# The order of calls in the ticks of every engine, drawn anew, in a software pipeline on one core

## What is computed

```python
x = x + rwkv_block(layernorm(x))     # 4 layers: time mix with a scan, channel mix 128 -> 512 -> 128
x = x + ffn(layernorm(x))            # gate, up 128 -> 352, down 352 -> 128, operands rounded to fp4
x = x + attention(layernorm(x))      # one causal head of 64 channels, softmax, output 64 -> 128
x = x + ffn(layernorm(x))

# in each layer of rwkv_block, k, v, r being products with mixes of h and h one token back:
#   out = (e1 * aa + e2 * v) / (e1 * bb + e2);  aa, bb: sums that decay, pp: their running maximum
# fp4: 16 neighbouring values share a scale, max|x| / 6, and are rounded to a grid of 8 magnitudes
```

## Time and profile before

| | us |
|---|---|
| time, median of 3 runs (1369.5 to 1373.78) | 1373.0 |
| span of the profiled execution (the time less what lies around it) | 1368.5 |
| PE busy | 1303.0 |
| ACT busy | 1257.6 |
| DVE busy | 1238.3 |
| POOL busy | 1122.6 |

### The profile page before, as it was taken

One profiled execution on the slowest core, in us unless ns is written; L12 is line 12 of the kernel. 1 busy time (PEld: TensorE's weight loads), 2 busy tenths in 40 slices (PEclk: granted clock), 3 DMA queues, 4 the chain that ended last, 5 costly groups with the idle time before them and its releaser, 6 DMA issues.

```text
span 1368.5 us, 23485 instructions
## 1 busy us (share of the span) xinstructions
PE 1303.0 (95%) x7285; PEld 935.9 (68%) x7285; DVE 1238.3 (90%) x2169; ACT 1257.6 (92%) x2539; POOL 1122.6 (82%) x1216
## 2 busy tenths in 40 slices
PE   3799999999999999999999999988999998899997
PEld 1356677667766677667766677766777876677776
DVE  6999999999999999999999999569999577978994
ACT  6899999999999999999999999877887899998884
POOL 6888998888888888888899999979998465666784
PEclk9899999999999999999999999999999999999999
DMA  7000000000000000000000000010000000000011
GB/s 237 1 1 1 1 1 1 1 21 13 1 0 2 1 1 1 1 1 1 1 1 1 8 24 21 27 32 1 1 1 1 2 1 1 1 16 16 24 32 39
DMA packets 26923, 18.54 MB, mean 14 GB/s; under 512 B 1072, under 2 KB 26160, under 8 KB 26800
## 3 DMA queue, kind: packets, MB, share of 16 engines
q1 hardware_dynamic: 26800, 17.05, 4.2%
HBM read 12.85 MB, written 4.19 MB: 12 GB/s over the span
## 4 chain that ended last, share of the span: by engine, by line
PE 67%; ACT 11%; DVE 9%; POOL 6%; issue 5%; DMA 0%; SPq 0%; DVEq 0%; ACTq 0%; POOLq 0%
PE ps L1154 12%; PE ps L1137 12%; PE ps L1213 5%; PE ps L1037 4%; PE ps L1192 4%; PE ps L1185 4%; PE ps L1144 3%; PE ps L1124 3%; PE ps L1089 3%; PE ps L1090 3%; PE ps L1102 3%; PE ps L1082 3%; PE ps L1263 3%; PE ps L1201 2%; PE ps L1245 2%
## 5 line engine op out<-in xcount | busy, mean ns | idle before, releaser
L1137 PE MATMUL ps<-xk,W 128*128 128x512 f32 x512 | 250.7, 593 | 1.4 <-ACT kf L864 1.4
L1154 PE MATMUL ps<-W,kf 128*128 128x128 f32 x2048 | 249.6, 275 | 0.0
L754 ACT ACTIVATE z<-X,ln_rs 128x128 f32<-128x128 f32 x512 | 239.7, 720 | 3.7 <-POOL ln_rs L603 3.7
L1154 PEld LDWEIGHTS ps<-W,kf 128*128 128x128 f32 x2048 | 239.2, 192 | 2.3 <-issue 1.0
L864 ACT ACTIVATE kf<-ps 128x512 f32<-128x512 f32 x256 | 186.6, 817 | 0.5 <-PE ps L1137 0.5
L871 ACT ACTIVATE kf<-kf 128x1024 f32<-128x1024 f32 x128 | 164.6, 1286 | 0.0
L1037 PEld LDWEIGHTS ps<-idn,z 128*128 128x128 f32 x664 | 83.1, 143 | 113.3 <-issue 87.3
L1137 PEld LDWEIGHTS ps<-xk,W 128*128 128x128 f32 x512 | 91.9, 190 | 92.1 <-issue 89.0
L710 POOL TENSOR_TENSOR W<-W,hsc 128x704 f32<-128x704 f32 x64 | 88.8, 1388 | 59.0 <-DVE W L493 58.8
L1037 PE MATMUL ps<-idn,z 128*128 128x128 f32 x664 | 102.0, 277 | 29.8 <-ACT z L754 20.7
L601 POOL TENSOR_TENSOR ln_rs<-ln_rs,mhalf 128x8 f32<-128x8 f32 (+1 forms) x70 | 127.9, 1827 | 0.0
(11 more groups left out here) (176 smaller groups left out, 3962.5 us busy)
## 6 DMA issues: line engine op xcount, KB each, us to landing
X<-x_in SPq DMA_DIRECT2D x16, 256.0 KB, 6.9
xi<-x_in SPq DMA_DIRECT2D x16, 256.0 KB, 2.9
out<-X SPq DMA_DIRECT2D x16, 256.0 KB, 2.3
W<-weights SPq DMA_DIRECT2D x4, 832.0 KB, 8.4
W<-fp4w SPq DMA_DIRECT2D x1, 560.0 KB, 3.8
row<-rows SPq DMA_DIRECT2D x1, 192.0 KB, 2.9
wqkv<-qkv SPq DMA_DIRECT2D x1, 96.0 KB, 5.7
idn<-ident SPq DMA_DIRECT2D x1, 64.0 KB, 3.1
```

The costliest lines, as they stand in the source:

```text
L754: last = e.activation(chunk(dst, j), chunk(src, j), ACT.Identity, bias=rs[:, 1, j:j + 1], scale=rs[:, 0, j:j + 1])
L1137: e.matmul((pF0, pF1)[f % 2][:, :], w_of(r, WCK + f), xk[r % 2][:, :], start=True, stop=True).then_inc(kf_mm[f], 1)
L1154: last = e.matmul(chunk(pKV, j), kf[r % 3][:, f, j * 128:(j + 1) * 128], w_of(r, WCV + f), start=f == 0 and j == 0, stop=f == 3, skip_grou ...
```

## The change

All functions stay as they are: the same instructions, tiles and waits. Drawn anew are the order of the calls in the four loops over ticks and, for some, the number taken off `t`. All loops now begin one tick earlier, at `FIRST = -1`, and end three earlier. Of the four tables two pieces stand here, the end of PE's old one and its successors in the new, and two edits of DVE's:

```diff
-TICKS = FFN2_AT + 35
+TICKS = FFN2_AT + 32
+FIRST = -1
...
-            for t in range(TICKS):
+            for t in range(FIRST, TICKS):
...
-                similarity(att_job(t - 6), 3)
-                a_turn(att_job(t - 4))
-                h_turn(ffn_job(t - 8), 2)
-                f_up(ffn_job(t - 5), 0)
-                p_values(att_job(t - 7))
...
+                p_values(att_job(t - 8))
+                output(t - 9)
+                f_gate(ffn_job(t - 6), 1)
+                f_up(ffn_job(t - 6), 0)
...
-                init_stats(t)
+                init_stats(t + 1)
```

More of the change, by code:

```diff
@@ L551, in vector @@
                 sub_d(t - 5)
[L552 removed]
+                rwkv(t - 7)
+                mul_up(ffn_job(t - 5), 1)
+                fh_add(ffn_job(t - 6), 0)
+                mix_k(t - 9)
                 bn2(t - 8)
[L554 to L561 removed]
@@ L575, in vector @@
-                prepare(t - 2)
-                weights_rounded(t - Q_AT - 3)
-                fh_scale(ffn_job(t - 5))
-                mix_k(t - 9)
-                fh_add(ffn_job(t - 6), 1)
+                mul_up(ffn_job(t - 5), 2)
+                fh_sub(ffn_job(t - 6), 0)
+                prepare(t - 3)
+                mul_up(ffn_job(t - 5), 3)
+                arg_r(t - 5)
+                a_mask(att_job(t - 5), 0)
+                fx_scale(ffn_job(t - 2))
+                a_max(att_job(t - 5), 0)
@@ new lines, in vector @@
+                fh_max(ffn_job(t - 5))
+                fx_inverse(ffn_job(t - 2))
+                fh_scale(ffn_job(t - 5))
+                mix_t(t - 4)
+                fh_add(ffn_job(t - 6), 1)
+                fh_inverse(ffn_job(t - 5))
+                fh_sub(ffn_job(t - 6), 1)
+                a_mask(att_job(t - 5), 1)
+                a_max(att_job(t - 5), 1)
+                init_stats(t + 1)
+                init_affine(t - 1)
+                a_inverse(att_job(t - 6))
+                a_mask(att_job(t - 5), 2)
@@ L585, in gpsimd @@
+                weights_scales(t - Q_AT + 18)
+                fx_max(ffn_job(t - 1))
+                gate(t - 11)
+                add_xa(t - 7)
+                a_add(att_job(t - 6))
+                bn1(t - 1)
+                fx_add(ffn_job(t - 2))
+                scan_pp(t - 4)
+                mul_up(ffn_job(t - 4), 0)
+                gated(t - 5)
+                fx_sub(ffn_job(t - 2))
+                mul_u(t - 6)
         def gpsimd():
@@ L722, in gpsimd @@
             constants()
-            for t in range(TICKS):
-                sub_dh1(t - 6)
-                add_res(ffn_job(t + 4))
-                mul_y(t - 9)
-                weights_divided(t - Q_AT - 2)
-                a_rsqrt(att_job(t - 5))
-                fh_scaled(ffn_job(t - 9), 0)
-                scaled_p(t - 9)
-                add_bias(att_job(t - 8))
-                add_num(t - 8)
-                fx_scaled(ffn_job(t - 6))
-                fx_divided(ffn_job(t - 5))
-                fh_divided(ffn_job(t - 8), 0)
-                fh_scaled(ffn_job(t - 9), 1)
-                add_den(t - 8)
-                add_xb(t - 14)
-                sub_dh(t - 11)
-                rsqrts(t - 4)
-                init_rsqrt(t - 2)
-                fh_divided(ffn_job(t - 8), 1)
-                f_rsqrt(ffn_job(t - 2))
-                weights_scaled(t - Q_AT - 5)
+            for t in range(FIRST, TICKS):
+                weights_divided(t - Q_AT - 5)
+                add_res(ffn_job(t - 2))
+                add_den(t - 16)
+                fx_scaled(ffn_job(t - 13))
+                sub_dh(t - 19)
+                add_bias(att_job(t - 14))
+                scaled_p(t - 16)
+                a_rsqrt(att_job(t - 11))
+                fh_scaled(ffn_job(t - 16), 0)
+                add_xb(t - 22)
+                rsqrts(t - 12)
+                weights_scaled(t - Q_AT - 19)
+                fx_divided(ffn_job(t - 12))
+                fh_divided(ffn_job(t - 15), 0)
+                fh_scaled(ffn_job(t - 16), 1)
+                f_rsqrt(ffn_job(t - 9))
+                mul_y(t - 16)
+                init_rsqrt(t - 9)
+                sub_dh1(t - 13)
+                fh_divided(ffn_job(t - 15), 1)
+                add_num(t - 15)
         def scalar():
@@ L982, in scalar @@
             prepare_vectors()
-            for t in range(TICKS):
+            for t in range(FIRST, TICKS):
+                square(t - 12, 0)
+                keep_hq(ffn_job(t - 9), 2)
+                fx_magic(ffn_job(t - 4))
+                norm1(t - 4)
+                silu(ffn_job(t - 6), 1)
+                tanh_r(t - 7)
+                square_1(t - 8)
+                fh_magic(ffn_job(t - 7), 0)
+                keep_h2(t - 10)
+                keep_fx(ffn_job(t - 5))
+                init_z(t - 1)
+                relu(t - 11, 1)
+                seeds(t - 7)
+                silu(ffn_job(t - 6), 2)
+                relu(t - 11, 2)
+                silu(ffn_job(t - 6), 3)
```

142 lines of the change are left out of this document (49 added, 93 removed).

## The result

The changed kernel takes 1419.99 us (median of 4, 1418.99 to 1423.17) against 1371.29 for the kernel before in the same comparison (median of 4): a ratio of 1.0353, 95% interval 1.0334 to 1.0372. The prediction was 1370.3 in a range of 1364.5 to 1379. The profiled execution has a span of 1418.9, 50.4 more than before.

A forecast was written before the change was run, and what follows sets the result against it. PE was taken to set the recurrent rounds, DVE the fill and first FFN, a ring of waits the join. Terms −4.7 + 1.9 − 1.1 + 0.5 + 0.7 + 0 = −2.7 on span 1368.5, plus 4.5: 1370.3 us, range 1364.5 to 1379.

The forecast's parts named there:

- Part 6: Recurrent rounds: PE's and ACT's sums unchanged and a new POOL–ACT ring of 12.84 under 13.11, so 0 us.
- the ring through POOL: Recurrent rounds: waits from ACT's h through POOL's sub_dh, two additions and root to ACT's norm2 and h; 12.84 us.
- the sign that the prediction named for being wrong: Recurrent rounds: a round longer than 13.11, with ACT's norm2 waiting for POOL's root.
- Rival B: Recurrent rounds: slower, the POOL–ACT ring sets the round; +7.5 beside −2.7, 1377.8 us, or about 1380; chance 0.18.
- point of decision: Recurrent rounds: the POOL–ACT ring sets the round if it is 0.3 us longer than summed.
- Part 1: Join of attention and second FFN: f_up 0 behind f_gate 1 shortens 8 ticks from 17.88 to 17.28; −4.7 us.
- Part 2: Start: DVE takes X2's statistics before the first affine and idles 1.7 longer for the transfer; +1.9 us.
- Part 3: From the rounds to the first FFN: fx_max moves into DVE's idle time and add_res comes a tick earlier; −1.1 us.
- the two terms of the forecast: Rounds to first FFN: fx_max in DVE's idle time, −0.6; POOL's add_res one tick earlier, −0.5.
- Part 4: DVE, FFN ticks: a lost gap between mul_up 3 and fh_max costs 0.04 in each of 24 ticks; +0.5 us.
- Part 5: Recurrent rounds: POOL's fp4 weight scaling, moved 4 to 6 ticks, overruns a round's slack once or twice; +0.7 us.

The follow-up runs named there:

- e10: The changed kernel with POOL's scaled_p moved from between sub_dh and the root to behind mul_y; 1418.56 us, ratio 1.0338.
- e5: The changed kernel with DVE's mix_rt moved directly behind mix_r, where POOL has its root; 1419.61 us, ratio 1.0337.
- e11: The changed kernel with the moves of e5 and e10 together, mix_rt beside the root and scaled_p behind mul_y; 1403.28 us, ratio 1.0227.
- e3: The kernel before with only PE's f_up 0 moved behind f_gate 1, for both FFNs; 1382.06 us, ratio 1.008.
- e7: The kernel before with PE's f_up 0 behind f_gate 1 and DVE's mul_up 0 behind fx_add, second FFN only; 1369.91 us, ratio 0.9973.
- s1: The kernel before with DVE's init_stats one tick earlier, so X2's statistics precede the first affine; 1373.95 us, ratio 1.0015.
- s2: The changed kernel with fx_scale moved behind mul_up 0 of the tick before, where POOL has the FFN's root; 1417.98 us, ratio 1.033.

## Why the prediction was wrong, point by point

The prediction said 1370.3, and the changed kernel takes 1420.0, 50 us more.

- **Part 6, the rounds: the step that failed.** It took 0 because the ring through POOL came to 12.84. The ring was the right one and every term but one was right within 0.1; add_xb was taken as "1.28 at most", from a row in which nothing met it, and had a slot of 1.81. With that the ring is 13.41, over PE's 13.05, as measured, and ACT's norm2 starts 0.08 behind the root, the sign that the prediction named for being wrong. The step also speaks of PE's and ACT's sums alone; for DVE the prediction had the premise that the same instructions in another order take the same time. That is false here: DVE's sum of a round rose by the meetings, to 13.34 in e10. Both limits are shown by e5, e10 and e11.
- **Rival B** named this ring and its point of decision, 0.3, and the rule of shared interfaces; it looked for the price at the root and not at the additions, and priced it at 0.15 a round for 50 rounds. The root as a whole kept its length: L601's row grew from 1.88 to 2.10 on average and L603's fell from 0.44 to 0.20, and sub_dh with the root takes 4.29 where the prediction had 4.32. The 0.36 in 35 rounds (13th to 48th aa) is 12.6 of the 16.1 lost there, and a round with weight work took 3.3 more. So B had the mechanism, and a fifth or less of the 50 us.
- **The fill**, from first to 13th aa, lost 10.9. DVE's SBUF-only instructions in that stretch are 12.7 us longer than in the trace before, while DVE was busy 163.9 of 165.7. Without scaled_p on the ring (e10, e11) the stretch is 159.9 to 160.0, half of the loss back; with mix_rt alone moved (e5) it is 166.4. No term was there for it.
- **Part 1, the join: right in size, half in reason.** −4.7 forecast, −5.6 measured; 17.28 forecast, 17.27 measured. But f_up 0 alone makes the kernel slower by 10, 7.6 of it in the join (e3): the prediction overlooked who waits for the moved call. The gain needs mul_up 0's move on DVE (e7), which the change also has.
- **Part 2, the start: right.** +1.9 forecast; +2.0 to 2.2 in the trace with the start alone (s1), +2.9 in the changed kernel, 0.1 over its bound.
- **Part 3, the seam: wrong sign.** −1.1 forecast, +7.0 measured between the 63rd aa and the first down. Of that 1.6 are in the 64th round and 1.1 in the first FFN ticks. About 1.8 may be the clock: the changed kernel's trace has 0.50 from 939.3 to 942.7, behind the turned weights, the trace before has 1.00 there, and s2's, also at 1.00, takes 72.2 and not 74.1 from the 63rd aa to the first long maximum. The other 2.5, and the two terms of the forecast, can't be told apart.
- **Part 4: mis-sized, then hidden.** A lost gap costs 0.11 to 0.12 (s2), not 0.04; in the changed kernel fx_scale stands in the gap, and with its meeting a tick costs 0.46 more: the stretches of the two FFNs lost 4.5 and 3.2.
- **Part 5, the weights: under-priced.** The changed kernel's rounds with weight work are 16.67, 14.63 and 19.73, 10.8 over three plain ones; the kernel before's are 14.49 and 16.65, 5.0 over two. One scale (L259, 128x70) takes 1.14 for 0.20. That DVE has no idle time left to hide this work is my reading, not tested. Together about 6 more, forecast +0.7.

Left open: half of the fill's loss, some 2.5 us at the seam, and a test of the ring in e11's last rounds.

## What to carry to other kernels

Before an order is called free, list for VectorE the instructions with two inputs in SBUF, and the one-input tensor_scalars, for GpSimd all that read SBUF, and see which stand beside each other: a sum of durations taken from a trace holds only for the neighbours of that trace. An edit that frees one limit of two shows little or nothing, so an unchanged time is no proof against its reason; make the second edit with it. When a producer is moved, look for its consumer's place in the other engine's queue: f_up alone cost 10 us, f_up with mul_up gained 3 to 4.
